# Turning u by VectorE in 32x32 blocks in an attention and FFN kernel on one core

## The chip, the cores and the metric

One core of one Trainium2 chip runs the whole program. The metric is the device time in microseconds (us), the median of several runs. TensorE multiplies, VectorE, ScalarE and GpSimd work on rows of 128 partitions, SyncE issues most DMAs. A profiled execution shows when each instruction ran and what ended the idle time before it. In rows of the profile PE is TensorE's products, PEld its weight loads, DVE VectorE, ACT ScalarE, POOL GpSimd, SPq the DMA queue of SyncE.

## What is computed

```python
# x [64, 64, 1024], c [64, 128]; all fp32
h   = gelu(gelu(c @ W0 + b0) @ W1 + b1);  att = softmax(h @ W2 + b2)         # [64, 8]
y   = einsum('boi,bih->boh', att @ weight, x) + (att @ bias_k)[:, :, None]   # a 64x64 mix of channels per batch
q, k, v = y @ Wq, y @ Wk, y @ Wv (+ biases)                                  # 32 heads of 32, one k and one v
p   = softmax(q[..., :, h] * k / sqrt(32));  o = sum_e p * v
x   = x + broadcast(o)                         # the kernel sums the heads of Wq: all heads give one row of 32
u   = conv1d(x, weight[64, 16, 9], groups=4, pad=4) + c @ c_weight.T + bias
out = x + u @ W.T + b                          # W: 1024x1024, unpacked from 4-bit values
```

## The kernel before

The 64 batches of 64 rows are cut into 16 **units** of 4 batches, each of two **tiles** of 128 rows (`TU = 2`, k = 2 x unit + tile). `project(a, t)` (L1074) multiplies unit a of `xt` with the 96 columns of q, v and k and gives z; ScalarE copies z to SBUF (`z_copy`); `mix(a)` (L1083) mixes its channels. VectorE then does the softmax of unit a, tile by tile: `softmax_top` (L792 to L813), `score` (L816), `subtract` (L821), the exponential on ScalarE (L573), `sum_exp` (L825), `times_v` (L829), `sum_v` (L833), `divide` (L837, L848), which gives `o`. SyncE saves `o` to DRAM (`save_o`, L306) and reads it back in another order into `o_c` (`spread_o`, L312, eight DMAs).

A **pass** p of the second half works on unit p-1 (passes 0 and 1 on two batches each, so that there are 17) in four **groups** g of 16 channels: GpSimd adds `o_c` to `xc` (`add_o`, L428 to L433), ScalarE makes the high part `c_hi` (`c_high`, L581), GpSimd or VectorE the rest `c_lo` (`c_low`, L441, L870), TensorE convolves (`conv`, L1098, six products), ScalarE copies with bias to `u_sb` (`u_copy`, L591). `u_sb` then has channel and position on the wrong axes for the FFN: `transpose_u` (L1109) makes four products with the identity (two in passes 0 and 1) into `p_ut`. ScalarE takes `u_hi` (`u_high`, L600) and VectorE `u_lo` (`u_low`, L875) from it. `linear(k, slot)` (L1114) is the FFN of tile k in eight slots of four products; slots 0 to 3 fill `p_f0`, 4 to 7 `p_f1`; its first product waits for all four `u_low` of its unit. `finish` (L884) adds `p_f` to `xn` on VectorE and so frees the bank; GpSimd has added `bias_n` and `o` to `xn` before (`x_bias` L452, `x_o` L459).

Each engine's order is written out by hand up to unit 2 of the FFN, and is a loop from there: TensorE's loop over d = 3 to 15 has 16 slots of `linear` with tables of slots in which convolutions and turns of pass d+2, `project(d+6)` and `mix(d+3)` stand; in VectorE's loop i the softmax is that of unit i = d+2. In this text **the start** is all before TensorE's loop (until 142.3 us), and a unit of the loop is **long** with a projection in it and **short** without. Waits are on semaphores (`s_u`: u copied, `s_ut`: turned, `s_uh`, `s_ul`: high and low taken, `s_o`: o ready, `s_res`: bank freed). The line that decides what a turn waits for:

```python
eng.wait_ge(s_u, G * p + g + 1)
if G * p + g >= 2:
    eng.wait_ge(s_ul, G * p + g - 1)
```

Of the kernel before, what the change touches and what calls it, by code (L numbers as in the profile page):

```python
# [13 lines left out]
P = 128  # L14
# [31 lines left out]
def block_program(nc, xt_in, xc_in, cols, mix_w, wq, wvk, conv_w, ctx_w, packed_t, xn_in, bias_in, out):  # L46
    ctx = ExitStack()
    with ctx:
# [194 lines left out]


# [30 lines left out]
        Z_SLOT = (0, 2)  # L275
        CONV_SLOT = (3, 5, 7, 9)
        UT_SLOT = (6, 8, 10, 12)
        MIX_SLOT = 6
# [4 lines left out]
        def _(eng):  # L283
# [81 lines left out]
            spread_o(2)  # L365
            save_o(3, 0)
            load_x(8)
            save_o(3, 1)
            spread_o(3)
            store(0)  # L370
            load_c(4)
# [12 lines left out]
            for i in range(5, NU + 2):  # L384
                d = i - 2
                store(TU * (d - 1) + 1)
                if i + 5 < NU:
                    load_x(i + 5)
                if i < NU:
                    save_o(i, 0)  # L390
                    save_o(i, 1)
                    spread_o(i)
                    if i < NU - 1:
                        load_c(i + 1)
                    load_n(i)
# [12 lines left out]
        def _(eng):  # L408
# [94 lines left out]
            x_bias(4)  # L503
            c_low(3, 3)
            x_bias(5)
# [15 lines left out]
            for p in range(5, NP):  # L521
# [8 lines left out]
                for t in range(TU):  # L530
                    x_bias(TU * unit_of(p) + t)
                    x_o(TU * unit_of(p) + t)

        @block.scalar
        def _(eng):
# [890 lines left out]
```

## Time and profile before

| | us |
|---|---|
| median of 3 runs | 457.26 (456.36 to 457.82) |
| the profiled execution | 457.46 |
| its span, first to last instruction | 455.7 |
| TensorE busy | 439.8 (97%) |
| VectorE busy | 332.6 (73%) |
| GpSimd busy | 342.2 (75%) |
| ScalarE busy | 225.1 (49%) |

The span is read as stretches. In the start the engines take turns in waiting. In the loop one unit is some 26.2 us (d = 3 to 9) or 22.6 us (d = 10 to 15). Busy shares are means over both; a wait counts for the end only where nothing else is late.

### The profile page before, as it was taken

The page shows a single profiled execution, that of the slowest core. Times are in us where ns is not written, and L with a number is a line of the kernel's source. Part 1 is how long each engine was busy: PE and PEld are TensorE (multiplying, and loading weights), DVE is VectorE, ACT ScalarE, POOL GpSimd, SP SyncE. Part 2 cuts the span into 40 slices and gives each one's busy share as a digit, 9 for nine tenths or more (in the row PEclk, how much of TensorE's full clock was granted, in tenths as well). Part 3 has the DMA queues.
Part 4 walks back from the last instruction along what each step waited for, and adds up shares of the span by engine and source line. Part 5 has one row for each costly group of instructions (what it writes and reads, how often), then busy time and mean ns, then how long its engine had stood idle before and what let it go on. Part 6 is the DMA issues. An engine that isn't in the chain of part 4 may idle for free.

```text
span 455.7 us, 7191 instructions
## 1 busy us (share of the span) xinstructions
PE 439.8 (97%) x2441; PEld 370.8 (81%) x2441; DVE 332.6 (73%) x538; ACT 225.1 (49%) x464; POOL 342.2 (75%) x314
## 2 busy tenths in 40 slices
PE   4989999999899999999999999999999999999997
PEld 3988997878688888888888888888888788888885
DVE  2999979985596768686776769677697979772121
ACT  3865625463454545535354453635555555563610
POOL 3085339795969996969879696987996999999910
PEclk9999999999899999999999999999999999999999
DMA  8999661414657583653919275542707280816112
GB/s 301 369 359 417 220 192 56 120 65 116 219 189 227 184 269 115 196 201 72 321 25 293 89 204 192 141 164 42 262 14 231 78 277 24 253 58 199 47 47 94
DMA packets 52595, 79.11 MB, mean 174 GB/s; under 512 B 38464, under 2 KB 38592, under 8 KB 48192
## 3 DMA queue, kind: packets, MB, share of 16 engines
q1 hardware_dynamic: 51168, 77.08, 51.0%
q10 hardware_dynamic: 1376, 1.31, 1.0%
q8 instruction: 36, 0.59, 0.5%
q14 instruction: 15, 0.12, 0.1%
HBM read 61.11 MB, written 17.27 MB: 172 GB/s over the span
## 4 chain that ended last, share of the span: by engine, by line
PE 73%; DMA 1%; POOL 1%; SPq 1%; issue 0%; DVE 0%; POOLq 0%
PE p_f L1114 46%; PE p_conv L1098 16%; PE p_sm L1074 5%; PE p_ut L1109 5%; PE p_sm L1083 1%; SPq L312 1%; DMA o_dram<-o_sb 1%; DMA o_c<-o_dram 0%; POOL xc L428 0%; POOL c_lo L441 0%; POOL xc L433 0%; POOL xc L431 0%; DVE xn L884 0%; DVE o_sb L848 0%; POOLq L457 0%
## 5 line engine op out<-in xcount | busy, mean ns | idle before, releaser
L1114 PE MATMUL p_f<-w_ffn,u_hi 128*128 128x512 f32 x512 | 203.3, 407 | 0.3 <-DVE xn L884 0.3
L1114 PE MATMUL p_f<-w_ffn,u_lo 128*128 128x512 f32 x512 | 198.7, 394 | 0.0
L591 ACT ACTIVATE u_sb<-p_conv,u_bias,cols_sb 128x128 f32<-128x128 f32 x256 | 96.5, 456 | 80.5 <-PE p_conv L1098 80.2
L1114 PEld LDWEIGHTS p_f<-w_ffn,u_hi 128*128 128x128 f32 x512 | 97.0, 189 | 19.6 <-issue 0.7
L1114 PEld LDWEIGHTS p_f<-w_ffn,u_lo 128*128 128x128 f32 x512 | 97.0, 189 | 18.7
L441 POOL TENSOR_TENSOR c_lo<-xc,c_hi 128x516 fp32r<-128x516 f32 (+1 forms) x66 | 82.1, 1249 | 36.8 <-ACT c_hi L581 18.6
L884 DVE TENSOR_TENSOR xn<-p_f,xn 128x512 f32<-128x512 f32 x64 | 44.2, 690 | 84.2 <-PE p_f L1114 84.2
L452 POOL TENSOR_TENSOR xn<-xn,bias_n 128x1024 f32<-128x1024 f32 x32 | 76.6, 2397 | 3.9 <-DMA xn<-xn_in_in 3.9
L428 POOL TENSOR_TENSOR xc<-xc,o_c 128x384 f32<-128x384 f32 x60 | 55.0, 917 | 27.6 <-DMA o_c<-o_dram 26.1
L581 ACT ACTIVATE c_hi<-xc 128x516 fp32r<-128x516 f32 (+1 forms) x68 | 41.5, 612 | 51.9 <-POOL xc L433 45.0
L459 POOL TENSOR_TENSOR xn<-xn,o_sb 128x1024 f32<-128x1024 f32 x30 | 57.4, 1918 | 2.0
L1098 PE MATMUL p_conv<-c_hi,cw_hi 128*128 128x512 f32 (+1 forms) x136 | 53.1, 391 | 3.7 <-POOL c_lo L441 2.3
L875 DVE TENSOR_TENSOR u_lo<-p_ut,u_hi 128x512 fp32r<-128x512 f32 (+1 forms) x68 | 44.2, 653 | 15.5 <-ACT u_hi L600 15.4
L1098 PE MATMUL p_conv<-c_hi,cw_lo 128*128 128x512 f32 (+1 forms) x136 | 52.3, 385 | 0.0
L1098 PE MATMUL p_conv<-c_lo,cw_hi 128*128 128x512 f32 (+1 forms) x136 | 52.3, 385 | 0.0
L1074 PEld LDWEIGHTS p_sm<-w,xt 128*128 128x128 f32 x416 | 49.9, 192 | 2.0 <-DMA xt<-xt_in_in 0.4
L600 ACT ACTIVATE u_hi<-p_ut 128x512 fp32r<-128x512 f32 (+1 forms) x68 | 39.1, 578 | 23.6 <-PE p_ut L1109 23.4
L1074 PE MATMUL p_sm<-w,xt 128*128 128x96 f32 x416 | 50.0, 273 | 0.3 <-DMA xt<-xt_in_in 0.3
L573 ACT ACTIVATE prob<-prob 128x1024 f32<-128x1024 f32 x32 | 34.0, 1062 | 27.9 <-DVE prob L821 27.8
L825 DVE TENSOR_REDUCE den<-prob 128x32 f32<-128x1024 f32 x32 | 38.8, 1211 | 2.5 <-ACT prob L573 2.5
L833 DVE TENSOR_REDUCE p_sm<-prob 128x32 f32<-128x1024 f32 x32 | 39.2, 1226 | 0.9
L829 DVE TENSOR_TENSOR prob<-prob,p_sm 128x1024 f32<-128x1024 f32 x32 | 38.9, 1218 | 0.8
(112 smaller groups left out, 483.6 us busy)
## 6 DMA issues: line engine op xcount, KB each, us to landing
xc<-xc_in_in SPq DMA_DIRECT2D x16, 1032.0 KB, 5.2
xn<-xn_in_in SPq DMA_DIRECT2D x16, 1024.0 KB, 8.4
out<-xn SPq DMA_DIRECT2D x31, 512.0 KB, 6.5
xt<-xt_in_in SPq DMA_DIRECT2D x15, 1024.0 KB, 6.0
o_c<-o_dram SPq DMA_DIRECT2D x116, 32.0 KB, 2.1
xn<-wq_in SPq DMA_DIRECT2D x4, 512.0 KB, 13.1
xt<-wq_in SPq DMA_DIRECT2D x1, 1024.0 KB, 7.6
xn<-wq_in SPq DMA_DIRECT2D x1, 1024.0 KB, 9.6
```

Of the source, the lines that this page charges most:

```text
L428: eng.tensor_tensor(x4[:, :, :, 0:3], x4[:, :, :, 0:3], o.unsqueeze(3).broadcast_to([P, UB, DH, 3]), ALU.add).then_inc(s_add, 1)
L441: eng.tensor_tensor(rows_of(c_lo, p, g), rows_of(xc[:, unit_of(p) % 2, :, :, :], p, g), rows_of(c_hi, p, g).bitcast(F32), ALU.subtract).th ...
L452: eng.tensor_tensor(x, x, bias_n[:, :], ALU.add).then_inc(s_xb, 1)
L459: eng.tensor_tensor(runs, runs, o_val(k).unsqueeze(2).broadcast_to([P, DH, D // DH]), ALU.add).then_inc(s_xo, 1)
L581: eng.activation(rows_of(c_hi, p, g), rows_of(xc[:, unit_of(p) % 2, :, :, :], p, g), ACT.Copy).then_inc(s_ch, 1)
L591: ins = eng.activation(u_sb[:, g % 2, i * P:(i + 1) * P], p_conv[g % 2][:, i * P:(i + 1) * P], ACT.Identity, bias=u_bias[:, g, bat:bat + 1 ...
L833: eng.tensor_reduce(num(a)[:, t, :], prob[:, t, :, :], AX.X, ALU.add).then_inc(s_num, 1)
L875: eng.tensor_tensor(ut_view(u_lo, p, g), columns(p_ut[g % 2], p).rearrange("p (n r c) -> p n r c", n=len(batches(p)), r=R), ut_view(u_hi, ...
L884: eng.tensor_tensor(x, p_f[half][:, :], x, ALU.add).then_inc(s_res, 1)
L1074: last = mm(z_ps(a)[:, t * W3:(t + 1) * W3], xt[:, a % NXT, r, t * P:(t + 1) * P], w3[:, r, :], start=(r == 0), stop=(r == R - 1))
L1098: last = mm(columns(p_conv[g % 2], p), w[:, shift, g, :], rows_of(src, p, g)[:, :, shift:shift + P], start=(n == 0), stop=(n == 5))
L1114: return mm(p_f[half][:, :], u[:, (k // TU) % 2, r, t * P:(t + 1) * P], w_ffn[:, r, 512 * half:512 * half + 512], **flags)
```

## The change

`transpose_u` on TensorE is gone. VectorE has `turn_u(p, g)`, with the same waits, which turns each block of 32x32 of `u_sb` in its place and writes `p_ut`: one instruction of 512 columns (256 in passes 0 and 1) for a group. Input channel 32a + b of the FFN then lies elsewhere, and the packed weights are laid out on the host in that order. `project` of units 9 to 15 no longer stands in d = 3 to 9 but, by the table `Z_AT`, in d = 3, 4, 6, 7, 9, 10, 11, ahead of the unit's first `linear`. All engines' orders are written anew.

```diff
-            return p_sm[(a + (a >= NZ)) % 2][:, TU * W3:2 * TU * W3]
+            return p_sm[a % 2 if a < NZ else (Z_AT[a] + 3) % 2][:, TU * W3:2 * TU * W3]
+        Z_AT = {7: 1, 8: 2, 9: 3, 10: 4, 11: 6, 12: 7, 13: 9, 14: 10, 15: 11}
-        Z_SLOT = (0, 2)
-        CONV_SLOT = (3, 5, 7, 9)
-        UT_SLOT = (6, 8, 10, 12)
-        MIX_SLOT = 6
...
@@ sync: the start
-            load_x(3)
             load_c(0)
-            load_bias()
+            load_c(1)
             eng.wait_ge(s_w3, 4)
             load_n(0)
-            load_c(1)
+            load_bias()
+            load_x(3)
...
             spread_o(2)
+            load_x(8)
             save_o(3, 0)
-            load_x(8)
             save_o(3, 1)
@@ sync: the loop
-                store(TU * (d - 1) + 1)
-                if i + 5 < NU:
-                    load_x(i + 5)
                 if i < NU:
                     save_o(i, 0)
                     save_o(i, 1)
+                if i - 3 in Z_AT.values() and unit_at(i - 3) + 2 < NU:
+                    load_x(unit_at(i - 3) + 2)
+                if i < NU:
                     spread_o(i)
...
+                store(TU * (d - 1) + 1)
+                if i < NU - 1:
+                    load_c(i + 1)
                 if d < NU:
                     store(TU * d)
+                if i < NU:
+                    load_n(i)
@@ scalar: the start
             u_copy(1, 1)
+            spread_half()
+            load_x6()
...
@@ scalar: the loop
                 u_copy(p, 1)
                 u_high(p, 0)
+                u_high(p, 1)
                 u_copy(p, 2)
-                u_high(p, 1)
                 u_copy(p, 3)
@@ vector
+            def turn_u(p, g):
+                eng.wait_ge(s_u, G * p + g + 1)
+                if G * p + g >= 2:
+                    eng.wait_ge(s_ul, G * p + g - 1)
+                else:
+                    eng.wait_ge(s_add, g + 2)
+                eng.transpose(columns(p_ut[g % 2], p), columns(u_sb[:, g % 2, :], p)).then_inc(s_ut, 1)
@@ tensor
-            def transpose_u(p, g):
...
-                for n in range(len(batches(p))):
-                    last = eng.transpose(p_ut[g % 2][:, n * P:(n + 1) * P], u_sb[:, g % 2, n * P:(n + 1) * P], ident[:, :])
-                last.then_inc(s_ut, 1)
...
+                if d in Z_AT.values():
+                    project(unit_at(d), 0)
+                    project(unit_at(d), 1)
+                linear(TU * d, 0)
...
+                linear(TU * d, 4)
+                if d + 1 < NU:
+                    conv(d + 2, 0)
+                linear(TU * d, 5)
+                if d + 3 < NU:
+                    mix(d + 3)
+                if d + 1 < NU:
+                    conv(d + 2, 1)
+                linear(TU * d, 6)
+                linear(TU * d, 7)
+                linear(TU * d + 1, 0)
+                if d + 1 < NU:
+                    conv(d + 2, 2)
+                    conv(d + 2, 3)
+                linear(TU * d + 1, 1)
...
-        "packed_t": arr("L0_ffn_packed_weight").T.reshape(P, R, HALF),
+        "packed_t": arr("L0_ffn_packed_weight").T.reshape(4, 32, 4, 2, HALF).transpose(2, 1, 0, 3, 4).reshape(P, R, HALF),
```

How the order changes on TensorE in the start, behind the mix of unit 0 (p_sm and p_f at L1074 and L1128 are the projections of units 1 and 2, the 64x129 products spread `o` of unit 0). Before:

```order
L1083 MATMUL p_sm<-z_own,mix_t 128x96 x2
L1074 MATMUL p_sm<-w,xt 128x96 x16
L1074 MATMUL p_f<-w,xt 128x96 x4
L1158 MATMUL p_ut<-cols_sb,u_sb 128x64 x4
L1074 MATMUL p_f<-w,xt 128x96 x16
L1228 TENSOR_LOAD flag
```

And now:

```order
L1137 MATMUL p_sm<-z_own,mix_t 128x96 x2
L1128 MATMUL p_f<-w,xt 128x96 x4
L1128 MATMUL p_sm<-w,xt 128x96 x4
L1128 MATMUL p_f<-w,xt 128x96 x4
L1128 MATMUL p_sm<-w,xt 128x96 x4
L1202 MATMUL p_ut<-cols_sb,u_sb 128x64 x4
L1128 MATMUL p_f<-w,xt 128x96 x4
L1128 MATMUL p_sm<-w,xt 128x96 x8
L1270 TENSOR_LOAD flag
```

The quarters of units 1 and 2 alternate, and unit 2 is first; three quarters of unit 3 have moved behind.

On VectorE in the loop, from the end of `softmax_top` to the next unit's first sum. Before:

```order
L813 TENSOR_TENSOR p_sm<-p_sm,top 128x64
L875 TENSOR_TENSOR u_lo<-p_ut,u_hi 128x4x8x16
L816 TENSOR_TENSOR prob<-p_sm,k_sb 128x1024
L875 TENSOR_TENSOR u_lo<-p_ut,u_hi 128x4x8x16
L821 TENSOR_TENSOR prob<-prob,p_sm 128x1024
L884 TENSOR_TENSOR xn<-p_f,xn 128x512
L875 TENSOR_TENSOR u_lo<-p_ut,u_hi 128x4x8x16 x2
L884 TENSOR_TENSOR xn<-p_f,xn 128x512
L816 TENSOR_TENSOR prob<-p_sm,k_sb 128x1024
L821 TENSOR_TENSOR prob<-prob,p_sm 128x1024
L825 TENSOR_REDUCE den<-prob 128x32
```

And now:

```order
L821 TENSOR_TENSOR p_sm<-p_sm,top 128x64
L889 STREAM_TRANSPOSE p_ut<-u_sb 128x512 x2
L902 TENSOR_TENSOR xn<-p_f,xn 128x512
L893 TENSOR_TENSOR u_lo<-p_ut,u_hi 128x4x8x16 x2
L824 TENSOR_TENSOR prob<-p_sm,k_sb 128x1024
L889 STREAM_TRANSPOSE p_ut<-u_sb 128x512
L829 TENSOR_TENSOR prob<-prob,p_sm 128x1024
L889 STREAM_TRANSPOSE p_ut<-u_sb 128x512
L893 TENSOR_TENSOR u_lo<-p_ut,u_hi 128x4x8x16
L902 TENSOR_TENSOR xn<-p_f,xn 128x512
L893 TENSOR_TENSOR u_lo<-p_ut,u_hi 128x4x8x16
```

Four turns have come between the softmax steps, two of them directly behind one another, and behind the next `finish` the sums of both tiles follow each other (two L833, two L837).

On SyncE in the loop, one unit. Before:

```order
L302 DMA out<-xn 128x1024 x2
L287 DMA xt<-xt_in_in 128x2048
L306 DMA o_dram<-o_sb 128x32 x2
L312 DMA o_c<-o_dram 16x16x32 x8
L297 DMA xc<-xc_in_in 128x2064
L292 DMA xn<-xn_in_in 128x2x1024
```

And now:

```order
L312 DMA o_dram<-o_sb 128x32 x2
L293 DMA xt<-xt_in_in 128x2048
L318 DMA o_c<-o_dram 16x16x32 x8
L308 DMA out<-xn 128x1024
L303 DMA xc<-xc_in_in 128x2064
L308 DMA out<-xn 128x1024
L298 DMA xn<-xn_in_in 128x2x1024
```

The load of `xt` stands between the save of `o` and its spreading; a store has moved behind them, and the load of `xn` to the end.

## Rows read from the trace of the kernel before

**Rows 1.** The page: busy us, share of the span and instructions of each engine.

```profile
PE 439.8 (97%) x2441; PEld 370.8 (81%) x2441; DVE 332.6 (73%) x538; ACT 225.1 (49%) x464; POOL 342.2 (75%) x314
```

**Rows 2.** Waits from 118 to 435 us: us in total, times, longest.

```profile
DVE xn L884 <- PE p_f L1114: 70.6, 43, 6.1
...
PE p_conv L1098 <- POOL c_lo L441: 2.0, 1, 2.0
```

**Rows 3.** Timeline of TensorE around one turn: start us, us, instruction.

```profile
344.63 0.39 PE L1114 MATMUL p_f<-w_ffn,u_lo 128*128 128x512 f32 x1
344.86 0.60 PE L1109 MATMUL p_ut<-ident,u_sb 128*128 128x128 f32 x4
...
345.53 0.40 PE L1114 MATMUL p_f<-w_ffn,u_lo 128*128 128x512 f32 x1
```

**Rows 4.** Groups by line and form: count | busy us, mean ns | idle before.

```profile
L875 DVE TENSOR_TENSOR u_lo<-p_ut,u_hi 128x512 fp32r<-128x512 f32 x60 | 41.0, 684 | 15.5 <-ACT u_hi L600 15.4
...
L1109 PE MATMUL p_ut<-ident,u_sb 128*128 128x128 f32 x256 | 38.7, 272 | 0.0
...
L875 DVE TENSOR_TENSOR u_lo<-p_ut,u_hi 128x256 fp32r<-128x256 f32 x8 | 3.3, 417 | 0.0
```

**Rows 5.** Windows of a long and a short unit: us, busy (count), clock, DMA, GB/s.

```profile
231.39:257.57 26.18, 26.18 (x141) 22.10 (x141) 19.58 (x32) 12.63 (x28) 21.24 (x20) 1.00 0.55 173
377.99:400.56 22.57, 22.57 (x110) 18.54 (x109) 19.44 (x32) 12.71 (x27) 21.67 (x22) 1.00 0.51 154
```

**Rows 6.** Timeline of VectorE in the short unit.

```profile
385.49 0.68 DVE L875 TENSOR_TENSOR u_lo<-p_ut,u_hi 128x512 fp32r<-128x512 f32 x1
386.09 1.22 DVE L816 TENSOR_TENSOR prob<-p_sm,k_sb 128x1024 f32<-128x1024 f32 x1
387.22 0.68 DVE L875 TENSOR_TENSOR u_lo<-p_ut,u_hi 128x512 fp32r<-128x512 f32 x1
...
389.83 0.69 DVE L884 TENSOR_TENSOR xn<-p_f,xn 128x512 f32<-128x512 f32 x1 [0.80 <-PE p_f L1114]
...
391.58 0.69 DVE L875 TENSOR_TENSOR u_lo<-p_ut,u_hi 128x512 fp32r<-128x512 f32 x1 [0.47 <-ACT u_hi L600]
393.72 0.69 DVE L884 TENSOR_TENSOR xn<-p_f,xn 128x512 f32<-128x512 f32 x1 [1.45 <-PE p_f L1114]
394.33 1.22 DVE L816 TENSOR_TENSOR prob<-p_sm,k_sb 128x1024 f32<-128x1024 f32 x1
395.58 1.22 DVE L821 TENSOR_TENSOR prob<-prob,p_sm 128x1024 f32<-128x1024 f32 x1
```

**Rows 7.** The second load of xt: timeline of TensorE, and DMA issues of 20 to 22 us.

```profile
22.11 0.66 PE L1083 MATMUL p_sm<-z_own,mix_t 128*128 128x96 f32 x4 [0.57 <-ACT z_own L565]
23.02 3.81 PE L1074 MATMUL p_sm<-w,xt 128*128 128x96 f32 x32 [0.26 <-DMA xt<-xt_in_in]
26.67 1.06 PE L1074 MATMUL p_f<-w,xt 128*128 128x96 f32 x8
...
21.56 0.33 SPq L287 DMA_DIRECT2D xt<-xt_in_in  x1
...
xt<-xt_in_in SPq DMA_DIRECT2D x1, 1024.0 KB, 4.8
```

**Rows 8.** TensorE behind its wait at 117.91 us, and the clock in a window there.

```profile
117.91 0.47 PE L1098 MATMUL p_conv<-c_hi,cw_hi 128*128 128x512 f32 x1 [1.99 <-POOL c_lo L441]
...
119.40 0.60 PE L1114 MATMUL p_f<-w_ffn,u_hi 128*128 128x512 f32 x1
...
122.79 0.43 PE L1114 MATMUL p_f<-w_ffn,u_hi 128*128 128x512 f32 x1
...
121.00:122.00 1.00, 1.00 (x4) 0.72 (x3) 0.97 (x2) 0.00 (x0) 1.00 (x2) 0.50 0.99 397
```

**Rows 9.** VectorE's waits from 22 to 118 us.

```profile
DVE u_lo L875 <- ACT u_hi L600: 6.4, 3, 2.9
DVE xc L864 <- DMA o_c<-o_dram: 2.7, 1, 2.7
```

More of the change, by code:

```diff
@@ L529, in _ @@
                 c_low(p, 3)
-                for t in range(TU):
-                    x_bias(TU * unit_of(p) + t)
-                    x_o(TU * unit_of(p) + t)
+                x_bias(TU * unit_of(p))
+                x_bias(TU * unit_of(p) + 1)
+                x_o(TU * unit_of(p))
+                x_o(TU * unit_of(p) + 1)
         @block.scalar
@@ L949, in _ @@
             divide(1, 1)
+            turn_u(1, 0)
             softmax_top(2)
[L951 to L952 removed]
+            u_low(0, 3)
             score(2, 0)
[L954 removed]
+            score(2, 1)
             subtract(2, 0)
             add_edges()
+            turn_u(1, 1)
+            subtract(2, 1)
+            sum_exp(2, 0)
+            u_low(1, 0)
+            c_low(2, 0)
+            turn_u(1, 2)
+            times_v(2, 0)
+            u_low(1, 1)
+            c_low(2, 1)
+            sum_v(2, 0)
+            turn_u(1, 3)
+            divide(2, 0)
+            sum_exp(2, 1)
             u_low(1, 2)
[L958 to L960 removed]
+            finish(0, 0)
             u_low(1, 3)
[L962 to L967 removed]
             times_v(2, 1)
[L969 removed]
+            turn_u(2, 0)
             sum_v(2, 1)
             divide(2, 1)
+            turn_u(2, 1)
+            finish(0, 1)
+            u_low(2, 0)
             softmax_top(3)
[L973 removed]
+            score(3, 0)
+            turn_u(2, 2)
             u_low(2, 1)
[L975 removed]
             finish(1, 0)
+            u_low(2, 2)
+            turn_u(2, 3)
             subtract(3, 0)
[L978 removed]
             u_low(2, 3)
             score(3, 1)
+            sum_exp(3, 0)
+            subtract(3, 1)
             finish(1, 1)
[L982 to L984 removed]
             times_v(3, 0)
+            sum_exp(3, 1)
             sum_v(3, 0)
[L987 removed]
+            times_v(3, 1)
             divide(3, 0)
[L989 removed]
             sum_v(3, 1)
             divide(3, 1)
+            turn_u(3, 0)
+            finish(2, 0)
+            turn_u(3, 1)
             softmax_top(4)
+            score(4, 0)
+            u_low(3, 0)
             finish(2, 1)
[L994 removed]
+            score(4, 1)
             u_low(3, 1)
[L996 to L997 removed]
+            turn_u(3, 2)
+            turn_u(3, 3)
             subtract(4, 0)
@@ L1024, in _ @@
                 a, b, d = i, i - 1, i - 2
-                finish(TU * d - 1, 1)
                 if a < NU:
@@ L1028, in _ @@
                     subtract(a, 1)
-                    attend(a, 0)
+                finish(TU * d - 1, 1)
+                if a < NU:
+                    sum_exp(a, 0)
+                    sum_exp(a, 1)
+                    times_v(a, 0)
+                    times_v(a, 1)
+                    sum_v(a, 0)
                 finish(TU * d, 0)
                 if a < NU:
-                    attend(a, 1)
-                finish(TU * d, 1)
+                    divide(a, 0)
+                    sum_v(a, 1)
+                    divide(a, 1)
                 if a + 1 < NU:
@@ L1036, in _ @@
                 if b < NU:
+                    turn_u(b + 1, 0)
+                    turn_u(b + 1, 1)
+                finish(TU * d, 1)
+                if b < NU:
                     u_low(b + 1, 0)
+                    u_low(b + 1, 1)
                 if a + 1 < NU:
@@ L1299, in _ @@
             linear(2, 2)
+            conv(3, 0)
             linear(2, 3)
```

279 lines of the change are left out of this document (117 added, 162 removed).

## Prediction

> **What bounds the kernel now.** I read the page's busy line first, then the waits, then the timeline of single units. The busy line gives TensorE 97% of the span [rows 1]. A busy TensorE need not be a bound, so the waits decide. From 118 us on, VectorE waits 70.6 us in total for TensorE's `p_f`, while TensorE waits once, 2.0 us for GpSimd [rows 2]. So from 118 us TensorE runs without a hole and each instruction taken out of its stream is worth its full time, as long as nobody else becomes late. Who could: in the windows of one unit [rows 5], 26.18 us long where TensorE also projects a later unit and 22.57 us where it doesn't, VectorE is busy 19.6 and 19.4 us, GpSimd 21.2 and 21.7 us. GpSimd and VectorE have room in a long unit and little in a short one. Before 118 us the picture differs: there VectorE too is nearly full, its largest waits being 6.4 us for `u_hi` and 2.7 us for `o_c` [rows 9].
>
> **Products removed.** A turn in the middle of the FFN is four products with the identity. In the timeline a product follows the last every 0.23 us; with a turn between, the product that would start at 345.09 (344.63 + 2 x 0.23) starts at 345.53 [rows 3]: 0.44 us for one group, not the 4 x 0.27 us of the busy column, since products overlap. Two of them (units of two batches) are taken as 0.22 us. Of the 256 records [rows 4], passes 5 to 16 of the loop hold 12 x 4 groups: 12 x 4 x 0.44 = **21.1 us**. The start holds 8 half groups and 12 full ones: 8 x 0.22 + 12 x 0.44 = **7.0 us**.
>
> **Turns added on VectorE.** No row shows a block transpose, so it is bounded. From below: it can't be under the half-size subtraction, 0.42 us for 256 columns, less the overlap, if it ran two columns at a time, 0.35 us. From above: one that passed every element twice would be twice the full subtraction, 1.3 us. The nearest row is the subtraction of `u_lo`, same engine, same 128x512 fp32 and the same bank, 0.68 us [rows 4]; the next instruction starts 0.60 us after it (385.49 to 386.09 [rows 6]). I take 0.60 us for a full turn, 0.33 for a half one. The Trainium skill weighs the other way (VectorE: DVE Perf Modes, "Rules for kernel authors": for a 128x128 transpose "Use TensorE if PSUM dest is OK"), and its table in "The three transpose paths" has 311 ns for a 128x128 bf16 one on VectorE; four of those are an estimate of 1.24 us a group, the heavy rival's price below, while as one instruction they would pay the fixed part once. No row here shows either.
>
> **The room for them.** In the window of 22.57 us VectorE has waits of 0.80, 0.47 and 1.45 us [rows 6], so a unit costs it 22.57 - 2.72 = 19.85 us. Four turns add 2.4. The new order puts the two tiles of the softmax alternately, which takes away gaps behind an instruction that needs its predecessor: what follows a score starts 1.13 us after it when it doesn't need it (386.09 to 387.22) and 1.25 us when it does (394.33 to 395.58) [rows 6]; four such gaps go, -0.5. Sum 21.75 us. TensorE's unit becomes 26.18 - 1.76 = 24.4 us with a projection and 22.57 - 1.76 = 20.8 without. VectorE is thus 2.7 us short of the long unit and 0.9 us over the short one. Before, units 3 to 9 were long and 10 to 13 short; now long ones stand at 3, 4, 6, 7, 9, 10, 11. The mean over units 3 to 13 is (7 x 24.4 + 4 x 20.8)/11 = 23.1 us, so VectorE fits in the mean, with 1.3 us a unit over, and no run of short units is longer than two while attention is still under way. GpSimd's 21.7 us fits in the mean too. What ties the units together inside: the last convolution now ends 6.5 us before the unit does (seven slots of 0.92), in which come four copies (1.5 us on ScalarE), the turn 0.6, `u_hi` 0.6, a `finish` 0.6 and `u_low` 0.6. That is about 4 us, 2 to 2.5 us left. I take no wait here. What queues behind a turn that waits: `finish`, which frees `p_f`; it has 3 to 6 us before TensorE opens that bank again. FFN inputs in the new order cost nothing: same products, same loads, same bytes. The DMAs that move with the orders (SyncE now spreads `o` ahead of the stores and loads) touch GpSimd's start, which has 21.7 of 23.1 us to do.
>
> **The start, where I expect a loss.** TensorE goes from one queue of work to another there. (a) It now projects unit 2 before unit 1. `xt` of unit 2 is issued at 21.56 us and lands 4.8 us later, 26.4; before, TensorE spent that time on unit 1 from 23.02 and took unit 2 at 26.67 [rows 7]. Now it waits from 22.8 to about 26.5: **+3.7 us**. (b) A wait like that was followed by a slow stretch in this trace: after the idle 1.99 us up to 117.91, the granted clock fell to 0.50, 1.2 GHz, and the eight products from 119.40 to 122.79 took 3.4 us in place of 8 x 0.23 = 1.9 [rows 8]. I add **+1.5 us**. (c) VectorE does the scores of both tiles before the first sum, and a third softmax step between; walking its list with the durations above I get the second tile of `o` of unit 0 at 42.1 us, some 3 us later than before, and TensorE reaches `copy_o(1, 0)` at about 41: **+1.2 us**. (d) The load of unit 6 stands on ScalarE behind a wait for `o` of unit 1, 1.8 us, and the projection of unit 5 waits 1.0 us for that `o`; against these, TensorE's own small waits of today go, some 2.5 us of the page's difference between its busy time and the span: **+0.3**. (e) The wait of 1.99 us at 117.91 came from a chain over `o` of unit 3; in the walk it vanishes, because the saves of `o` no longer have a load between them, and with it its slow stretch: **-3.5 us**. Sum with the 7.0 removed: -7.0 + 3.7 + 1.5 + 1.2 + 0.3 - 3.5 = **-3.8 us**. VectorE's own sum in the start: 8 x 0.33 + 12 x 0.60 = 9.8 us of turns, against waits of 6.4 + 2.7 = 9.1 us before 118 us [rows 9], of which the first kind, for products behind other work on TensorE, goes with them. That is tight, and why I don't count on more.
>
> **Sum.** The profiled execution took 457.46 us (span 455.7 and 1.8 around it), 0.2 over the median of 457.26. 457.46 - 21.1 - 3.8 = 432.6; I say **432.5 us**. The tail, the last unit's FFN, is unchanged.
>
> **Rivals.**
> - *The start gives all or nearly all of its 7 us* (no slow stretch after the first wait, and the small waits hidden): 457.46 - 28.1 + 0 to 1 = 429 us. For it: TensorE's list there has much independent work. Against: the transfer at 26.4 us can't come earlier. Chance 0.12.
> - *Hand-over latencies.* In short units TensorE stands at the first product of the next unit until `u_low` of group 3, because the chain of 4 us starts late once VectorE lags. Four short units at 1 to 1.5 us, plus two slow stretches as in [rows 8]: 432.5 + 5 = 437.5 us. For it: VectorE is 0.9 us over a short unit. Against: it enters one with 2.7 us in hand. Chance 0.15.
> - *Heavy turns.* At 1.15 us each VectorE's unit is 19.35 + 4.6 = 24.0 us, 0.9 over the mean of TensorE: 11 x 0.9 = 10 us, and 12 x 0.55 + 8 x 0.28 = 9 us more VectorE work in a start that has little room, of which half shows: 432.5 + 14.5 = 447 us. VectorE becomes the bound from 0.94 us a turn on ((23.1 - 19.35)/4). For it: its two-pass bound. Against: the 0.68 us row. Chance 0.12. By the estimate of 1.24 us from the Trainium skill's page above (VectorE: DVE Perf Modes) it would be 451 us.
> - *Slower than before.* One mechanism: block turns that move an element in three steps, 3 x 0.53 = 1.6 us. VectorE's unit would be 25.8 us, 2.7 over the mean: 11 x 2.7 = 30 us there and 12 x 1.0 + 8 x 0.5 = 16 us in the start, nearly all of which shows: 477 us. It decides from about 1.38 us a turn, where VectorE's unit reaches today's mean of (7 x 26.18 + 4 x 22.57)/11 = 24.9 us. Only the lack of any row speaks for it. Chance 0.04.
> - *It doesn't do what it says*: TensorE's time doesn't fall, since the products hid in weight loads. The gap of 0.44 us a group in [rows 3] speaks against. 457 us, chance 0.02.
>
> **How the numbers follow.** The forecast has 0.55. Its own range is 430.5 to 435. With the first two rivals 0.82 is covered by 428.5 to 441; the heavy turns and what is beyond (0.18) are left out. A measurement of this kernel tells 0.3%, 1.4 us, from no change. Faster by more than that: all but the last two, 0.94; within it 0.02; slower 0.04.
>
> **What would show it.** In the new trace: the turn at 0.65 to 0.72 us; units from one first convolution to the next of 24.4 us with a projection and 20.8 without; VectorE's wait for `p_f` between 118 us and the end down from 70.6 to 30 us or less; TensorE idle from 22.8 to 26.5 us, the clock at 0.50 for some 3 us behind it; no wait near 117 us. It is wrong if TensorE waits for VectorE's `u_lo` or `p_f` banks by more than 5 us in all, or if the turn takes over 0.94 us.

## The result and the profile after

The changed kernel takes **433.9 us** (median of 4 runs, 433.03 to 434.89) against 457.54 of the kernel before, run on the same chip (median of 4). The ratio is 0.947, 95% interval 0.9408 to 0.9532. The forecast was 432.5 us, the range 428.5 to 441. The profiled execution took 433.03 us, its span is 430.9.

The page of the changed kernel: the busy line, which answers to [rows 1], and the granted clock in 40 slices.

```profile
PE 412.5 (96%) x2185; PEld 347.8 (81%) x2185; DVE 365.2 (85%) x606; ACT 224.5 (52%) x464; POOL 341.2 (79%) x314
...
PEclk9969899999999999999999999999999999999999
```

TensorE has 27.3 us less to do, VectorE 32.6 us more, and the span fell by 24.8 us. The groups of VectorE by shape, answering to [rows 4] (busy us, mean ns of one | idle before):

```profile
L902 DVE TENSOR_TENSOR xn<-p_f,xn 128x512 f32<-128x512 f32 x64 | 43.4, 678 | 22.8 <-PE p_f L1158 22.4
L889 DVE STREAM_TRANSPOSE p_ut<-u_sb 128x512 f32<-128x512 f32 x60 | 42.5, 714 | 18.2 <-ACT u_sb L600 18.2
L893 DVE TENSOR_TENSOR u_lo<-p_ut,u_hi 128x512 fp32r<-128x512 f32 x60 | 39.4, 672 | 0.3 <-ACT u_hi L609 0.3
```

The turn takes 0.714 us beside 0.672 for the subtraction. What it costs VectorE is the time to the next instruction; the timeline of VectorE in a short unit:

```profile
362.11 1.31 DVE L889 STREAM_TRANSPOSE p_ut<-u_sb 128x512 f32<-128x512 f32 x2
363.32 0.67 DVE L902 TENSOR_TENSOR xn<-p_f,xn 128x512 f32<-128x512 f32 x1
...
369.76 0.67 DVE L893 TENSOR_TENSOR u_lo<-p_ut,u_hi 128x512 fp32r<-128x512 f32 x1
```

Two turns in 363.32 - 362.11 = 1.21 us: 0.605 each. Windows of a long and of a short unit, each from one first convolution to the next, answering to [rows 5] (length, busy time of each engine with its instructions, granted clock, DMA share, GB/s):

```profile
286.00:310.32 24.32, 24.32 (x125) 20.55 (x124) 21.58 (x36) 13.36 (x28) 23.60 (x22) 1.00 0.47 144
355.36:376.07 20.71, 20.71 (x93) 16.97 (x92) 20.43 (x36) 12.34 (x26) 19.31 (x19) 1.00 0.50 152
```

TensorE is busy for the whole of both. The long unit fell from 26.18 to 24.32 us, the short one from 22.57 to 20.71. The waits from 118 us to the end, answering to [rows 2]:

```profile
DVE xn L902 <- PE p_f L1158: 22.4, 11, 3.2
...
DVE p_ut L889 <- ACT u_sb L600: 17.1, 19, 6.9
...
POOL xc L436 <- DMA o_c<-o_dram: 6.5, 6, 1.6
```

VectorE's wait for `p_f` went from 70.6 to 22.4 us. TensorE itself has from 72.8 us on a single wait, 0.69 us at 399.57 for `c_lo`. The loop starts at 138.8 us in place of 142.2 (its first product starts at 142.17 in the trace of before; the text ahead of the prediction has 142.3). Nearly all that TensorE loses, it loses in the start; its waits from 20 to 140 us and the windows with the granted clock (third number from the right):

```profile
PE p_f L1128 <- DMA xt<-xt_in_in: 3.6, 1, 3.6
PE p_f L1217 <- DVE o_first L850: 1.4, 1, 1.4
PE p_sm L1128 <- DMA xt<-xt_in_in: 1.1, 1, 1.1
PE p_conv L1152 <- POOL c_lo L449: 1.0, 2, 0.7
PE p_sm L1137 <- ACT z_own L574: 0.6, 1, 0.6
PE p_conv L1152 <- DVE c_lo L878: 0.3, 1, 0.3
```

```profile
22.00:27.00 5.00, 1.38 (x8) 1.22 (x9) 4.93 (x12) 2.13 (x1) 4.67 (x1) 0.66 0.88 326
27.00:30.00 3.00, 3.00 (x16) 3.00 (x16) 2.96 (x4) 2.11 (x2) 2.91 (x3) 0.50 1.03 429
...
33.00:44.00 11.00, 8.69 (x82) 7.25 (x82) 8.68 (x22) 7.99 (x15) 4.00 (x4) 1.00 0.95 353
44.00:50.00 6.00, 6.00 (x48) 5.40 (x49) 6.00 (x10) 4.33 (x10) 4.30 (x4) 0.72 0.68 279
```

The clock falls to its lower level, 1.2 GHz, behind the wait of 3.6 us for the transfer, and a second time behind the wait of 1.4 us for `o`.

### The profile page after: what moved, and what is told of

Same layout as the page of the kernel before. It is cut to its first block and busy times, and to the rows that moved or that the text cites. A ratio compares the mean times of both kernels' runs of the same rounds, so it can differ in the third digit from the quotient of the medians.

```text
span 430.9 us, 6747 instructions
## 1 busy us (share of the span) xinstructions
PE 412.5 (96%) x2185; PEld 347.8 (81%) x2185; DVE 365.2 (85%) x606; ACT 224.5 (52%) x464; POOL 341.2 (79%) x314
## 5 line engine op out<-in xcount | busy, mean ns | idle before, releaser
L1158 PE MATMUL p_f<-w_ffn,u_hi 128*128 128x512 f32 x512 | 196.0, 393 | 0.0
L1158 PE MATMUL p_f<-w_ffn,u_lo 128*128 128x512 f32 x512 | 194.7, 390 | 0.0
L600 ACT ACTIVATE u_sb<-p_conv,u_bias,cols_sb 128x128 f32<-128x128 f32 x256 | 94.9, 460 | 40.3 <-PE p_conv L1152 39.8
L449 POOL TENSOR_TENSOR c_lo<-xc,c_hi 128x516 fp32r<-128x516 f32 (+1 forms) x66 | 82.3, 1256 | 22.2 <-ACT c_hi L590 14.7
L436 POOL TENSOR_TENSOR xc<-xc,o_c 128x384 f32<-128x384 f32 x60 | 54.5, 908 | 23.6 <-DMA o_c<-o_dram 22.4
L902 DVE TENSOR_TENSOR xn<-p_f,xn 128x512 f32<-128x512 f32 x64 | 43.4, 678 | 22.8 <-PE p_f L1158 22.4
L889 DVE STREAM_TRANSPOSE p_ut<-u_sb 128x512 f32<-128x512 f32 (+1 forms) x68 | 46.1, 683 | 18.2 <-ACT u_sb L600 18.2
L1152 PE MATMUL p_conv<-c_hi,cw_hi 128*128 128x512 f32 (+1 forms) x136 | 54.6, 401 | 2.0 <-POOL c_lo L449 1.6
L609 ACT ACTIVATE u_hi<-p_ut 128x512 fp32r<-128x512 f32 (+1 forms) x68 | 39.2, 578 | 33.2 <-DVE p_ut L889 28.4
L1128 PEld LDWEIGHTS p_sm<-w,xt 128*128 128x128 f32 x416 | 49.9, 194 | 2.6 <-DMA xt<-xt_in_in 1.3
L1128 PE MATMUL p_sm<-w,xt 128*128 128x96 f32 x416 | 50.2, 277 | 1.1 <-DMA xt<-xt_in_in 1.1
L893 DVE TENSOR_TENSOR u_lo<-p_ut,u_hi 128x512 fp32r<-128x512 f32 (+1 forms) x68 | 42.6, 641 | 0.3 <-ACT u_hi L609 0.3
L833 DVE TENSOR_REDUCE den<-prob 128x32 f32<-128x1024 f32 x32 | 37.9, 1211 | 2.0 <-ACT prob L582 2.0
```

What stands on the lines that cost most here:

```text
L436: eng.tensor_tensor(x4[:, :, :, 0:3], x4[:, :, :, 0:3], o.unsqueeze(3).broadcast_to([P, UB, DH, 3]), ALU.add).then_inc(s_add, 1)
L449: eng.tensor_tensor(rows_of(c_lo, p, g), rows_of(xc[:, unit_of(p) % 2, :, :, :], p, g), rows_of(c_hi, p, g).bitcast(F32), ALU.subtract).th ...
L600: ins = eng.activation(u_sb[:, g % 2, i * P:(i + 1) * P], p_conv[g % 2][:, i * P:(i + 1) * P], ACT.Identity, bias=u_bias[:, g, bat:bat + 1 ...
L889: eng.transpose(columns(p_ut[g % 2], p), columns(u_sb[:, g % 2, :], p)).then_inc(s_ut, 1)
L893: eng.tensor_tensor(ut_view(u_lo, p, g), columns(p_ut[g % 2], p).rearrange("p (n r c) -> p n r c", n=len(batches(p)), r=R), ut_view(u_hi, ...
L902: eng.tensor_tensor(x, p_f[half][:, :], x, ALU.add).then_inc(s_res, 1)
```

## The experiments

The time was as forecast. Whether for the reasons given is another matter: the sum mixed the turns, the new orders and a start full of small terms. The first four runs take these apart, the next four test size and order, and the last four ask what sets the start. Times are medians of 4 to 10 runs, compared with 433.9 us, or on the last chip with 434.2. The changed kernel itself was not run on the chips of runs 1 to 4 and 5 to 8; the kernel before took 455.5 us on the first and 456.8 on the second, against 457.54 where the 433.9 were measured. So a difference of one or two microseconds between chips tells nothing by itself.

### 1. The turns of the loop back on TensorE

```diff
                 linear(TU * d, 6)
+                if d + 1 < NU:
+                    transpose_u(d + 2, 0)
                 linear(TU * d, 7)
+                if d + 1 < NU:
+                    transpose_u(d + 2, 1)
...
-                    turn_u(b + 1, 0)
-                    turn_u(b + 1, 1)
```

> The changed kernel with one thing undone: in the loop (units of passes 5 to 16) the turns are products with the identity again, 48 groups of four, put between the slots of the FFN as the kernel before had them; the start, the new orders and the spread z stay. (The FFN of these units then meets its weights in the other order of the inputs; the work is the same.) Theory: each group is worth 0.44 us of TensorE's stream, 48 x 0.44 = 21.1 us, so 433.9 + 21.1 = 455 us, with units of 26.1 us (projection) and 22.5 us (none) in place of 24.3 and 20.7. Rival: the new orders and the spread of z brought most of the 23.6 us and the turns little; then 433.9 to 442 us, with TensorE's larger sum paid by waits that go. In between would mean that new waits eat part of the gain of the turns.

Measured: 456.85 us (456.04 to 459.69), 23 us more. The same two units in the trace of this run:

```profile
300.10:326.20 26.10, 26.10 (x141) 22.10 (x140) 19.26 (x32) 12.86 (x27) 21.05 (x22) 1.00 0.43 134
375.00:397.50 22.50, 22.50 (x109) 18.53 (x108) 19.05 (x32) 12.53 (x26) 21.03 (x21) 1.00 0.50 154
```

26.10 and 22.50 us are the 26.1 and 22.5 of the theory, and about what the units of the kernel before had. TensorE waits 1.7 us for `u_sb` ahead of turns; the rest of the 23 us, some 21, is 48 groups of 0.44 us. The new orders and the spread z, with block turns in the start alone, are worth nothing: 456.85 against 455.5 of the kernel before on this chip (ratio 1.0022, 0.9992 to 1.0052). The rival is out.

### 2. Only the turns of the start back on TensorE

The 20 `turn_u` lines of VectorE's start are taken out, and `transpose_u(p, g)` stands on TensorE behind the first or second item after its convolution, for instance:

```diff
             linear(0, 6)
+            transpose_u(1, 3)
             project(6, 1, 1)
             linear(0, 7)
+            transpose_u(2, 0)
```

> The changed kernel with only the turns of the start (passes 0 to 4, 8 half groups and 12 full ones) as products with the identity again, each put right after a convolution or a slot of the FFN by which its input is ready; the loop keeps its turns on VectorE. (The FFN of the first units meets its weights in the other order; the work is the same.) Theory: 8 x 0.22 + 12 x 0.44 = 7.0 us of TensorE's stream come back, and since TensorE there waits only for a transfer and for o, not for turns, nearly all shows: 433.9 + 6 to 7 = 440 to 441 us, the loop starting at 145 to 146 us in place of 138.8. Rival: VectorE's chain sets the start, so TensorE has room for them: at most +3 us, 434 to 437.

Measured: 451.08 us (450.63 to 452.22), 17 us more, and the loop starts near 159 us. Both answers were too small. TensorE's waits from 20 to 150 us in this run:

```profile
PE p_ut L1143 <- DVE u_lo L893: 5.2, 2, 4.0
PE p_f L1108 <- DMA xt<-xt_in_in: 3.6, 1, 3.6
PE p_conv L1132 <- POOL c_lo L449: 3.3, 3, 2.4
PE p_ut L1143 <- ACT u_sb L600: 3.1, 2, 2.6
...
```

8.3 us of waits stand in front of the turns themselves and 2.3 us more in front of convolutions; with the 7.0 us of products that is 17.6. Behind the longest of these waits, 3.96 us up to 76.39, the granted clock is 0.50 from 76 to 80 us. A turn on TensorE holds up everything queued behind it, while it waits for a copy and for the subtraction two groups back. I placed these turns, and other places may wait less, so the run doesn't price the move in the start; it shows only what these turns cost in these places.

### 3. Each turn twice

```diff
+                eng.transpose(columns(p_ut[g % 2], p), columns(u_sb[:, g % 2, :], p)).then_inc(s_dup, 1)
+                eng.wait_ge(s_dup, G * p + g + 1)
                 eng.transpose(columns(p_ut[g % 2], p), columns(u_sb[:, g % 2, :], p)).then_inc(s_ut, 1)
```

> The changed kernel with each block turn made twice, the second on the same data and after the first has ended: about 0.72 + 0.61 = 1.33 us a turn in place of 0.61 to the next instruction. It prices the heavy-turn rival of the prediction. By the prediction's sums: VectorE's unit is 21.75 + 4 x 0.7 = 24.6 us against 23.0 us, the mean of TensorE's units, 1.6 us over, 11 x 1.6 = 17 us, and half of 12 x 0.7 + 8 x 0.4 = 11.6 us in the start: 433.9 + 17 + 6 = 457 us; VectorE's waits for p_f from 138 us on go to nearly nothing and TensorE waits for u_lo. Rival A: VectorE's idle time counts whole, 30 us in the loop by its waits, so 48 x 0.7 = 34 us cost only some 5 us there: 442 us or less. Rival B: the turns stand in the chain convolution, copy, turn, subtraction, product, so each of the 48 hand-overs is late by its length: over 465 us.

Measured: 458.72 us (457.8 to 459.03); the sums had 457. The windows of a long unit, of ten units together and of a short unit, then TensorE's wait from 140 us on:

```profile
303.60:328.10 24.50, 24.50 (x126) 20.65 (x125) 24.08 (x40) 12.43 (x28) 21.17 (x21) 1.00 0.44 142
156.70:403.10 246.40, 236.32 (x1113) 195.23 (x1112) 242.18 (x393) 124.89 (x268) 214.39 (x205) 0.97 0.53 168
378.70:403.10 24.40, 22.54 (x93) 17.98 (x92) 23.98 (x40) 12.33 (x26) 21.06 (x21) 0.93 0.45 143
```

```profile
PE p_f L1161 <- DVE u_lo L896: 10.5, 5, 3.5
```

The ten units from the convolution at 156.7 to that at 403.1 take 24.6 us each in place of 22.9, which is 17 us; the start takes 10 us more, the end 1 less. VectorE waits for nothing in these ten units, so 24.6 us is its own unit (theory: 24.6). Measured at TensorE's convolutions single units differ, from 22.3 to 27.0 us, but a long and a short one can now last the same, as above. The second turn starts 0.75 us after the first (288.25 after 287.50 in its timeline), and with it the whole gain of 23.6 us is gone.

VectorE's waits in the same ten units of the changed kernel (146.93 to 376.07 us):

```profile
DVE p_ut L889 <- ACT u_sb L600: 7.1, 13, 0.7
DVE qkv_bias L800 <- PE p_sm L1137: 2.7, 5, 0.5
DVE xn L902 <- PE p_f L1158: 2.5, 3, 0.8
```

The sum fits: 40 second turns of 0.75 us are 30 us, these waits take up 12.3 of them, and 17.7 are left.

### 4. Unit 1 projected before unit 2

```diff
-            project(2, 0, 0)
             project(1, 0, 0)
-            project(2, 0, 1)
             project(1, 0, 1)
...
+            project(2, 0, 0)
             context()
+            project(2, 0, 1)
```

> The changed kernel with unit 1 projected ahead of unit 2 at the start, as the kernel before had it; nothing else moves. Theory (terms a and b of the prediction): TensorE's wait of 3.62 us for xt of unit 2 at 26.2 us and the slow stretch behind it go, 3.7 + 1.5: 433.9 - 5 = 429 us, the loop starting at 133.6 in place of 138.8 us. Rival: the wait was cover for VectorE's chain (scores of unit 0, then o); TensorE then stands at copy_o(1, 0) or at a convolution instead and less than 1.5 us is gained: 432.5 to 434 us.

Measured: 433.2 us (432.27 to 434.23). The wait of 3.62 us and the slow stretch behind it are gone, and 0.7 us is gained, within what can be told from none. In its trace TensorE waits instead 1.92 us for `o_first` at 33.2, 1.02 us for it at 43.2 and 2.77 us at 60.0 for the `xt` of unit 5 (1.15 before). The rival holds. The clock's fall has moved too: granted clock 1.00 where the old slow stretch was, 0.62 and 0.50 behind the wait of 1.92 us, 0.70 behind that of 2.77.

```profile
27.00:33.00 6.00, 3.48 (x30) 3.15 (x28) 5.84 (x7) 5.21 (x8) 4.94 (x3) 1.00 1.02 418
33.00:36.00 3.00, 2.77 (x20) 2.07 (x20) 2.76 (x4) 1.65 (x3) 0.75 (x1) 0.62 1.01 414
36.00:39.00 3.00, 3.00 (x18) 2.51 (x16) 2.12 (x10) 1.42 (x2) 1.50 (x2) 0.50 1.01 408
...
62.00:66.00 4.00, 4.00 (x20) 3.75 (x19) 3.20 (x4) 2.03 (x4) 1.64 (x1) 0.70 0.89 242
```

### 5. The old orders with the block turns

The kernel before, with `turn_u` put into VectorE's old order and `transpose_u` taken from TensorE's; in the loop:

```diff
                 if b < NU:
+                    turn_u(b + 1, 0)
+                    turn_u(b + 1, 1)
                     u_low(b + 1, 0)
...
                     u_low(b + 1, 1)
+                    turn_u(b + 1, 2)
```

> The kernel before with one thing changed: the turns are made by VectorE, each put one or two instructions ahead of its subtraction in VectorE's old order, and the FFN inputs are in the order of the block turns; every other order and the projections of units 9 to 15 in passes 3 to 9 stay as they were. With the run in which only the turns of the loop went back it gives the share of the orders. Theory: the turns alone would give 457.3 - 21.1 - 7.0 = 429 us if VectorE kept up; with the old orders it does not, since passes 10 to 13 are four short units of 20.8 us in a row against VectorE's 22.2 (19.85 + 4 x 0.60), 4 x 1.4 = 5.6 us, and in the start its idle 10 us before 118 us are not where the turns fall, another 3 to 5: 438 to 441 us. Rival: the orders are worth nothing or little with the turns either: 432 to 435 us.

Measured: 448.33 us (446.02 to 451.43), 14 us more than with the new orders and 7 more than I had thought. The four executions lie in two pairs, near 446 and near 451, so the 14 us are known to some 3 us; the trace is of one at 446.15. A long and a short unit, then TensorE at the end of that short one:

```profile
274.50:299.50 25.00, 24.61 (x125) 20.46 (x124) 21.93 (x35) 12.63 (x27) 21.18 (x20) 1.00 0.46 140
343.30:365.60 22.30, 21.01 (x93) 16.89 (x92) 21.75 (x36) 12.49 (x27) 21.10 (x21) 1.00 0.51 151
```

```profile
359.96 0.39 PE L1149 MATMUL p_f<-w_ffn,u_lo 128*128 128x512 f32 x1
361.64 0.50 PE L1149 MATMUL p_f<-w_ffn,u_hi 128*128 128x512 f32 x1 [1.29 <-DVE u_lo L885]
```

and VectorE there:

```profile
359.12 0.70 DVE L881 STREAM_TRANSPOSE p_ut<-u_sb 128x512 f32<-128x512 f32 x1
359.73 0.67 DVE L894 TENSOR_TENSOR xn<-p_f,xn 128x512 f32<-128x512 f32 x1
360.32 1.27 DVE L885 TENSOR_TENSOR u_lo<-p_ut,u_hi 128x512 fp32r<-128x512 f32 x2
```

The short unit has 22.3 us, VectorE's pace as the expectation had it (22.2), for 20.71 with the new orders. The long ones, where I had no loss, have 25.0 for 24.32: TensorE stands 0.4 us at each first product of a unit for the last `u_low`, the hand-over that the prediction had as a rival; the other 0.3 us was not taken apart. Six long and five short units make 259.8 us for 249.4, which is 10.4; the start makes 2.4. In the changed kernel the same `u_low` starts at 369.76 and ends at 370.43, while the unit's first product is due at 376.07 - 5 x 0.92 = 371.5: 1.1 us in hand where the old order is 1.3 late. So the orders are worth nothing while the loop's turns are on TensorE (run 1), and some 14 us as soon as they are on VectorE.

### 6. The projections of units 9 to 15 in a row

```diff
-        Z_AT = {7: 1, 8: 2, 9: 3, 10: 4, 11: 6, 12: 7, 13: 9, 14: 10, 15: 11}
+        Z_AT = {7: 1, 8: 2, 9: 3, 10: 4, 11: 5, 12: 6, 13: 7, 14: 8, 15: 9}
```

> The changed kernel with units 9 to 15 projected in passes 3 to 9 in a row, as before, in place of 3, 4, 6, 7, 9, 10 and 11; all else stays. Passes 10 to 13 are then four short units in a row. Theory: VectorE needs 21.8 us a unit and TensorE 20.7 in them, so 4 x 1.1 = 4.4 us less what VectorE is ahead on entering (up to 3 us): 433.9 + 1.5 to 3 = 435.5 to 437 us, as waits of TensorE for u_lo in passes 11 to 14. Rival: VectorE's lead covers all of it, 433.5 to 434.5 us.

Measured: 436.23 us (433.96 to 437.45), 2.3 us more, in the theory's bounds. The mechanism isn't shown, since the profiled execution was the shortest one (433.96), and in it TensorE waits only 0.24 us for `u_lo` and 1.5 us for `c_lo` late in the run. Its third and fourth short units in a row:

```profile
333.60:354.30 20.70, 20.70 (x94) 16.96 (x93) 20.42 (x35) 11.87 (x26) 19.74 (x19) 1.00 0.47 140
354.30:375.60 21.30, 21.06 (x94) 16.90 (x93) 21.02 (x36) 12.42 (x26) 20.68 (x20) 1.00 0.56 180
```

VectorE is full, and only the fourth unit in a row is held up. In this execution its lead is larger than I had allowed.

### 7. The clock kept up through both waits

```diff
             mix(0)
+            keep_busy(p_conv[0], 15)
             project(2, 0, 0)
...
+                    if p:
+                        eng.wait_ge(s_add, G)
+                        keep_busy(p_f[0], 6)
                     eng.wait_ge(s_o, p + 1)
```

> The changed kernel with products on ones, which nobody reads, put into TensorE's two waits of the start: 15 ahead of the projection of unit 2 (the wait for its xt, 3.62 us up to 26.18) and 6 ahead of copy_o(1, 0) (the wait for o, 1.35 us up to 43.89). They are to keep the clock: after both waits the trace of the changed kernel shows a stretch at half speed (granted clock 0.66 and 0.50 from 22 to 30 us, 0.72 from 44 to 50). Theory: both slow stretches go, 1.5 + 1 us, and TensorE is that much earlier from there on: 431.5 us. Rival: VectorE's chain over o and the load of unit 5's xt set the start; TensorE comes earlier to its next wait and waits longer there: 433.5 to 434.3 us, with the clock at 1.00.

Measured: 433.32 us (431.96 to 433.84), and the clock stays at its upper level:

```profile
27.00:33.00 6.00, 6.00 (x57) 6.00 (x55) 5.93 (x6) 3.40 (x6) 5.27 (x3) 1.00 1.02 425
...
44.00:50.00 6.00, 6.00 (x56) 5.42 (x56) 5.64 (x12) 4.82 (x10) 3.01 (x3) 1.00 0.64 261
```

The rival holds. TensorE starts on unit 5's `xt` 2.6 us earlier (57.94 for 60.58) and then waits 0.65 us for a copy at 67.94, 1.07 for `c_lo` at 71.74, 0.71 at 96.54 and 0.66 at 147.43, all for other engines. The two slow stretches cost next to nothing.

### 8. A turn and a quarter

```diff
+                if p >= 5:
+                    eng.transpose(p_ut[g % 2][:, 0:P], u_sb[:, g % 2, 0:P]).then_inc(s_dup, 1)
+                    eng.wait_ge(s_dup, G * (p - 5) + g + 1)
```

> The changed kernel where each of the 48 turns of the loop is preceded by a turn of its first 128 columns, made again by the whole turn: VectorE pays about 0.25 + 0.1 us more a turn, 0.95 in place of 0.61, right at the point of 0.94 us from which the prediction has VectorE become the bound. Theory: its unit becomes 21.75 + 4 x 0.35 = 23.15 us against the mean of 23.0, so nearly nothing is lost: 434 to 436 us. Rival: hand-overs inside the unit, each late by the longer turn, cost from the first tenth on: 48 x 0.3 = 14 us, or half of it, 441 to 448 us.

Measured: 435.63 us (433.24 to 437.79), 1.7 us more. The rival of 14 or 7 us is out. The rows of one such turn:

```profile
322.47 0.30 DVE L891 STREAM_TRANSPOSE p_ut<-u_sb 128x128 f32<-128x128 f32 x1
322.80 0.73 DVE L893 STREAM_TRANSPOSE p_ut<-u_sb 128x512 f32<-128x512 f32 x1
323.44 0.67 DVE L897 TENSOR_TENSOR u_lo<-p_ut,u_hi 128x512 fp32r<-128x512 f32 x1
```

0.97 us a turn (322.47 to 323.44) costs nearly nothing, 0.63 + 0.75 us costs 25. The threshold lies close to the 0.94 us of the prediction: VectorE's waits in the ten units of the loop are down from 12.3 to 1.7 us, and TensorE waits just once in the loop for `u_lo`, 0.97 us at 372.55. The trace is of the fastest execution (433.24), so where the median's 1.7 us go is not shown.

### 9 to 12. What sets the start

After runs 4 and 7 I formed the theory that VectorE does, since it is busy 109 of the 118 us from 22 to 140. Four kernels on one chip: the changed one, one with VectorE relieved, one with TensorE's waits mended, and one with both.

> The changed kernel itself, as the yardstick for the next three on the same chip: 433 to 435 us.

```diff
-                eng.tensor_tensor(prob[:, t, :, :], prob[:, t, :, :], along(qkv(a)[:, t, DH:2 * DH]), ALU.mult).then_inc(s_pv, 1)
+                n = DH // 2 if 1 <= a <= 4 else DH
+                eng.tensor_tensor(prob[:, t, 0:n, :], prob[:, t, 0:n, :], along(qkv(a)[:, t, DH:2 * DH])[:, 0:n, :], ALU.mult).then_inc(s_pv, 1)
```

> The changed kernel with less VectorE work in the start: the product of the exponentials with v of units 1 to 4 covers half of prob (its second half goes unmultiplied into the sum), 8 instructions of about 0.6 us in place of 1.13, so 4.2 us less. Nothing of TensorE, of the transfers or of the orders moves. Theory (formed after the two runs on TensorE's side): VectorE's chain sets the start; it is busy 109 of the 118 us from 22 to 140. Then 433.9 - 3 to 4 = 430 to 431 us, the loop starting near 135.5 in place of 138.8 us. Rival: TensorE's stream and the transfers set it, and VectorE is merely full: gain under 1 us.

```diff
+            keep_busy(p_conv[0], 7)
             eng.wait_ge(s_flag, 1)
...
             project(3, 1, 0)
-            project(4, 0, 0)
             project(3, 1, 1)
+            project(4, 0, 0)
```

> The changed kernel with all that I know on TensorE's side of the start mended, VectorE's list untouched: unit 1 projected first (no wait of 3.62 us for xt of unit 2), 7 products on ones that nobody reads ahead of copy_o(0, 0) and 6 ahead of copy_o(1, 0) to keep the clock, and the last quarter of unit 3's projection one place earlier, so that its buffer is free for unit 5's load some 2 us earlier (the wait of 1.15 us at 60.58). Theory that VectorE's chain sets the start: within 1 us of the changed kernel, 432.9 to 434. Rival: these waits each cost what they last: -3.7 - 2.5 - 1.1, so 427 us.

> The last two edits together (half of prob left unmultiplied for units 1 to 4, and TensorE's side mended). Theory: with VectorE's chain shortened by 4.2 us, TensorE's waits begin to count, and the two edits together bring more than the sum of each alone: 427 to 429.5 us. Rival: they don't add, 430 to 431 us, since GpSimd's c_lo or the transfers of o come next.

| | median us | lowest to highest | against the changed kernel |
|---|---|---|---|
| changed kernel again | 434.2 | 433.27 to 435.13 | |
| VectorE relieved | 433.14 | 431.89 to 435.1 | -1.1 |
| TensorE's side mended | 432.67 | 431.18 to 433.59 | -1.5 |
| both | 431.2 | 430.27 to 431.69 | -3.0 |

My theory fell. 4.2 us less VectorE work is worth 1.1 us, which can't be told from nothing; TensorE's waits and slow stretches (7.3 us by the rival's sum) 1.5, at the edge of that; and together they bring 3.0, which is clear of noise, about their sum and not much more. In the third kernel one slow stretch is left, granted clock 0.84 from 39 to 50 us around a wait of 1.48 us; in the fourth the clock is 1.00 there. So neither VectorE's work nor TensorE's waits set the start alone. In the run with both, TensorE's remaining waits name several others:

```profile
PE p_f L1113 <- DVE xc L865: 1.5, 1, 1.5
PE p_conv L1153 <- POOL c_lo L449: 1.0, 1, 1.0
PE p_ut L1203 <- DMA u_sb<-ctx_w_in: 0.8, 1, 0.8
...
```

The second, GpSimd's `c_lo` at 144.21, stands already in the loop: TensorE starts the loop there at 134.9 us, 3.9 earlier than in the first trace of the changed kernel, and waits for GpSimd once it is there. How the rest divides among VectorE, GpSimd and the copies stays open. The third kernel leaves nothing out, and its ratio to the kernel before is 0.9476 (0.945 to 0.9502) against 0.9521 (0.9496 to 0.9546): a little better than the change, at the edge of what can be told.

## Why the prediction was right, and where it was not

- **Products removed, 21.1 us in the loop.** Right. The units fell by 1.86 us each in the windows, 0.46 a group, where 4 x 0.44 = 1.76 was counted, and run 1 gives 23 us back for 48 groups, 1.7 of them waits.
- **The turn at 0.60 us.** Right: 0.605 to the next instruction, 0.714 by its record (forecast 0.65 to 0.72). The nearest row, the subtraction in [rows 4], was the right guide. The estimate of 1.24 us from the Trainium skill (VectorE: DVE Perf Modes, "The three transpose paths"), made of four single 128x128 turns, is twice what one instruction of 512 columns takes. The Trainium skill's advice (VectorE: DVE Perf Modes, "Rules for kernel authors"), "Use TensorE if PSUM dest is OK", is given for a full 128x128 transpose, which the block turn is not. Followed here, it would have left the work on the engine that was the bound (run 1: 23 us). By run 3 the price did decide: at some 1.4 us a turn nothing is left.
- **VectorE's unit of 21.75 us and the threshold of 0.94.** Right. In the changed kernel ten units take 229.1 us, of which VectorE waits 12.3: 21.7 us a unit. Run 3, bound by VectorE, has 24.6 us, which less 4 x 0.75 for the second turns is 21.6. Run 5 shows a short unit of 22.3 with the old order and no wait of VectorE in it, so the gaps that the new order saves are some 0.6 us a unit, where 0.5 was counted. At 0.63 + 0.75 = 1.38 us a turn run 3's unit without turns is 24.6 - 4 x 1.38 = 19.1 us, and (22.9 - 19.1)/4 puts the threshold at 0.95. Run 8, at 0.97 us a turn, loses 1.7 us.
- **The units at 24.4 and 20.8 us.** Measured 24.32 and 20.71, without a wait of TensorE. That VectorE may fall back in a short unit and catch up in a long one was right. The room behind the last convolution was there, but in that short unit it was 1.1 us at 370.43, not 2 to 2.5.
- **The orders.** The prediction gave them only the gaps (-0.5 us a unit) and the spread of z. Run 5 shows them to be worth some 14 us with the turns on VectorE: of the 23.6 us gained, 14 hang on them. The spread of z is about 2 us of that by the median of run 6; its trace doesn't show them. The rest, by the rows of run 5, is VectorE's shorter unit and `u_low` ending ahead of the product that needs it; these two were not taken apart. The rival of hand-over latencies describes the old orders, not the new ones.
- **The start, -3.8 us.** The loop starts 142.2 - 138.8 = 3.4 us earlier, and most of its terms were there: 3.62 us of wait (3.7 forecast), a slow stretch behind it, 1.35 us for `o` (1.2), no wait near 117 us. Term (d) was not: of its 1.8 us for unit 6 and 1.0 us for `o`, the first doesn't show, and in place of the second stand 1.15 us for unit 5's `xt`. Left out was the second slow stretch, from 44 to 50 us. But the step that fails is the adding itself. It describes one trace, and the terms are not costs: without the 3.62 us and the slow stretch behind it the kernel gains 0.7 us, since other waits and slow stretches come up (run 4), without both slow stretches 0.6 (run 7), with nearly all of it mended 1.5. Nor is it shown that the products removed there are worth their 7.0 us; run 2 put them back in places where they also wait. From 22 to 140 us TensorE is busy 111 of 118 us, VectorE 109, GpSimd 82 and ScalarE 63, and the first two also wait for each other, for GpSimd and for transfers. The sum came out right, in part by luck, its reason didn't.
- **The end.** A wait of 0.69 us at 399.57 for a chain over `o`, its way through DRAM and GpSimd was not foreseen.

## What to carry to other kernels

Before work is moved to a half idle engine, work out that engine's time per unit against the bound's mean unit, and the price per instruction from which it becomes the bound: forecast 0.94 us, it came out at 0.95 by run 3, and 0.97 us cost nearly nothing in run 8. Then look at the hand-over inside the unit, for the order decides whether the room in the mean can be used: the same move gave some 8.5 us with the old order (448.33 from 456.8) and 23.6 with the new one. And don't add up an engine's waits in a stretch where the engines wait for one another in turn; take one away on the chip before pricing it.

## What the hardware showed

- VectorE's turn of 32x32 blocks of fp32 from SBUF to PSUM costs like a subtraction of the same size: 714 ns for 512 columns, 449 ns for 256 (8 in the changed kernel) and some 0.30 to 0.33 us for 128, so about 1.03 ns a column and 0.19 us fixed.
- TensorE's clock fell to its lower level (0.50 from 45 to 47 us, 0.72 as the mean from 44 to 50) behind a wait of only 1.35 us, at the end of 11 us of small instructions in which TensorE was busy for 8.7. With products on ones ahead of this wait and of the earlier one it stayed at 1.00 (run 7). In the loop of run 5 it stayed at 1.00 behind a wait of 1.29 us, up to 361.64; there TensorE had been busy for all of 343.3 to 360.0 us.
- Keeping the clock up bought nothing that can be told here (433.32 against 433.9 us), since what followed waited for others.
